# A feed-forward pass run over four chunks in two groups instead of over two chunks

## The chip, the cores and the metric

One Trainium2 chip, one core of it. The metric is device time in microseconds (us). The engines are TensorE (PE, matmuls; its weight loads are PEld), VectorE (DVE), ScalarE (ACT), GpSimd (POOL) and SyncE (SP, which here issues all DMAs). All arithmetic of this pass is in 32-bit floats.

## The reference

128 images are cut into 196 patches each, embedded to 256 features, and a class token is put in front: 197 tokens of 256. Then one layer: h + attention(layernorm(h)), and h + ffn(layernorm(h)). The feed-forward part is not the usual one:

```
global_context = x.mean(axis=1, keepdims=True)
gf = _global_net(global_context, ...)            # 256 -> 128 -> 64 -> 1, gelu, gelu, sigmoid
out = x
for _ in range(NUM_CYCLES):                      # 3
    tf = _coupling_net(out, ...)                 # 256 -> 256 -> 128 -> 64 -> 1, gelu x3, sigmoid
    combined = 0.7 * gf + 0.3 * tf
    coupling = BASE_COUPLING + adaptive_range * (combined - 0.5) * 2.0
    out = out + coupling * _twist(out)           # signed swap of the two halves of the features
return out
```

## The kernel before

The kernel has two passes. The first (embedding, attention, residual) goes image by image and writes its result to a DRAM scratch; the change leaves its code alone. The second pass is the feed-forward part. It works on **chunks** of two images: 2 x 197 = 394 columns (N2), features on the 128 partitions in two halves f. 64 chunks are taken in 32 **pairs**; c is 0 or 1.

Each engine has its own in-order program, written out by hand; semaphores tie them together, and nothing is scheduled by a planner. A chunk goes through these steps:

- SP loads the chunk twice from the scratch: `hl` for the norm, `hk` for the residual (L381).
- DVE `stats2` (L907, L911), POOL `norm2` (L525, L527), DVE `apply2` (L920) make the layer norm `hn2`.
- PE `x_transpose` (L1278) and ACT `x_copy` (L539) put it as `X`, features on partitions.
- DVE `gsums` (L925), then the global net: PE L1287, L1291, L1292 with ACT L649, L652, L655, and DVE `alphas` (L930).
- Three cycles of: layer 1 (PE L1307, eight records of two passes each for four matmuls), gelu (ACT L663); layer 2 (L1316), gelu (L667); layer 3 (L1321, 128 to 64), gelu (L671); layer 4 (L1325, 64 to 1, the weight column repeated 128 times so that every partition gets the result), tanh (L675). Then DVE `update`: four `base` instructions (L942) that don't need the tanh, and u (L946), new first half (L952), u (L953), new second half (L956).
- PE `y_transpose` (L1338), DVE `finish` (L965) adds it to `hk`, SP stores it (L391).

Chunk 1 runs about half a cycle behind chunk 0: PE does layers 3 and 4 of chunk 1 between layers 1 and 2 of chunk 0. Each chunk owns four of the eight PSUM banks. The order on each engine is that of its `pass2`, called for each pair.

## Time and profile before

| | us |
|---|---|
| median of 3 runs | 4073.27 |
| lowest, highest | 4049.71, 4074.95 |
| the profiled execution | 4066.9 |
| its span, first to last instruction | 4065.1 |
| PE busy | 3857.1 (95%) |
| DVE busy | 3042.6 (75%) |
| ACT busy | 2481.0 (61%) |
| POOL busy | 1818.8 (45%) |

The first pass ends near 2612 us. The rest is the second pass: a start of some 24 us in which the first two chunks are loaded and normed, and 32 pairs. Busy times of engines overlap and don't add up; which engine others wait for shows in the waits and in the timeline.

### The profile page before, as it was taken

What the parts mean: (1) busy time and instruction counts of PE and PEld (TensorE: products, weight loads), DVE (VectorE), ACT (ScalarE), POOL (GpSimd) and SP (SyncE); (2) the same over time, 40 slices, a digit from 0 to 9 for tenths busy, and PEclk for the clock granted to TensorE, in tenths of its full rate; (3) what the DMA queues carried; (4) which work ended last, traced back from release to release, by engine and by line L of the source; (5) the groups of instructions that cost most, each with busy time, mean ns of one, the idle gap of its engine ahead of it and who ended that gap; (6) DMA issues with size and microseconds to landing.
All of it is one profiled execution on the core that took longest, in us unless ns stands there. A gap on an engine that the chain in (4) does not pass through costs nothing.

```text
span 4065.1 us, 84521 instructions
## 1 busy us (share of the span) xinstructions
PE 3857.1 (95%) x29966; PEld 2761.4 (68%) x29966; DVE 3042.6 (75%) x7327; ACT 2481.0 (61%) x5890; POOL 1818.8 (45%) x2960
## 2 busy tenths in 40 slices
PE   6999999999999999999999999699999999999998
PEld 5888888888888888888888887444444444444444
DVE  6777777777777777777777777477777767777776
ACT  4777777777777777777777777444444444444443
POOL 3666666666666666666666666300000000000000
PEclk9999999999999999999999999799999999999999
DMA  3444444444444444444444444311112112111211
GB/s 106 127 127 127 122 122 123 126 127 124 125 128 128 123 122 122 124 128 126 126 128 126 122 123 105 83 48 57 48 60 59 50 52 60 56 48 60 60 49 40
DMA packets 199842, 398.21 MB, mean 98 GB/s; under 512 B 28032, under 2 KB 133760, under 8 KB 199424
## 3 DMA queue, kind: packets, MB, share of 16 engines
q1 hardware_dynamic: 199424, 392.81, 36.0%
q8 instruction: 242, 3.96, 0.4%
q14 instruction: 176, 1.44, 0.1%
HBM read 131.80 MB, written 53.26 MB: 46 GB/s over the span
## 4 chain that ended last, share of the span: by engine, by line
PE 81%; DVE 7%; issue 3%; ACT 3%; POOL 3%; DMA 2%; SPq 0%; DVEq 0%; POOLq 0%; ACTq 0%
PE ps L1307 13%; PE ps L1027 13%; PE ps L1316 7%; PE ps L1114 7%; PE ps L1062 6%; PE ps L1075 5%; PE ps L1325 4%; PE ps L1141 4%; PE ps L1321 3%; PE ps L1122 3%; PE ps L1099 3%; DVE mx L855 3%; PE ps L1148 3%; DVE mx L851 2%; PE ps L1143 2%
## 5 line engine op out<-in xcount | busy, mean ns | idle before, releaser
L1027 PE MATMUL ps<-xb,w_tok 128*128 128x196 f32 x3072 | 694.8, 350 | 0.8 <-DVE h L767 0.5
L851 DVE TENSOR_REDUCE mx<-ps 128x4 f32<-128x512 f32 x512 | 352.6, 689 | 362.6 <-PE ps L1143 362.6
L525 POOL TENSOR_SCALAR ve<-mv 128x4 f32<-128x4 f32 x64 | 14.9, 233 | 1286.8 <-DVE mv L911 1286.8
L1307 PE MATMUL ps<-X,cn_w 128*128 128x394 f32 x1536 | 552.6, 502 | 0.0
L855 DVE TENSOR_REDUCE mx<-ps 69x2 f32<-69x396 f32 x1024 | 528.8, 556 | 0.0
L545 ACT ACTIVATE p<-ps 128x394 f32<-128x394 f32 x1024 | 454.9, 499 | 78.1 <-PE ps L1075 68.6
L1027 PEld LDWEIGHTS ps<-xb,w_tok 128*128 128x128 f32 x3072 | 487.0, 190 | 1.2 <-DVE h L767 0.8
L663 ACT ACTIVATE a<-ps,cn_b 128x394 f32<-128x394 f32 x384 | 226.6, 590 | 368.4 <-PE ps L1307 354.8
L496 POOL TENSOR_TENSOR h<-h,att 128x256 f32<-128x256 f32 (+1 forms) x256 | 188.2, 755 | 533.3 <-DVE att L844 533.3
L1307 PEld LDWEIGHTS ps<-X,cn_w 128*128 128x128 f32 x1536 | 280.3, 191 | 176.3 <-issue 3.0
L1148 PE MATMUL ps<-kZ,qT 128*69 128x396 f32 x1024 | 398.4, 455 | 0.1
L1075 PE MATMUL ps<-qZ,kT 128*128 128x396 f32 (+1 forms) x2048 | 379.2, 318 | 12.9 <-DMA qZ<-mx_scratch 10.1
L457 POOL TENSOR_SCALAR_AFFINE_SELECT p<-p 128x512 f32<-128x512 f32 x512 | 372.1, 727 | 7.8 <-ACT p L545 7.8
L563 ACT ACTIVATE sq<-ps 128x256 f32<-128x256 f32 (+1 forms) x512 | 196.1, 383 | 280.9 <-PE ps L1062 280.8
L471 POOL TENSOR_TENSOR qkv<-qkv,wk_row 128x256 f32<-128x256 f32 (+1 forms) x256 | 229.3, 896 | 255.2 <-DVE qkv L819 255.2
L1075 PEld LDWEIGHTS ps<-qZ,kT 128*128 128x128 f32 (+1 forms) x2048 | 307.7, 167 | 39.6 <-issue 16.9
L1316 PE MATMUL ps<-a,cn_w 128*128 128x394 f32 x768 | 304.3, 518 | 10.4 <-DVE hk L965 6.3
L539 ACT ACTIVATE qkv<-ps 128x512 f32<-128x512 f32 (+1 forms) x512 | 306.3, 598 | 0.0
L539 ACT ACTIVATE qT<-ps 128x396 fp32r<-128x396 f32 x512 | 228.1, 499 | 118.2 <-PE ps L1114 118.1
L946 DVE SCALAR_TENSOR_TENSOR u<-X,c_tf,th 128x394 f32<-128x394 f32 x192 | 119.8, 624 | 224.9 <-ACT th L675 224.9
L1062 PE MATMUL ps<-w_qkv,hnT 64*128 64x256 f32 (+1 forms) x2048 | 284.0, 396 | 0.5 <-ACT hnT L539 0.5
L1099 PE MATMUL ps<-p,qkv 128*17 128x197 f32 x4096 | 254.1, 334 | 24.3 <-POOL p L461 18.9
(140 smaller groups left out, 8784.9 us busy)
## 6 DMA issues: line engine op xcount, KB each, us to landing
kZ<-kT SPq DMA_DIRECT2D x512, 198.0 KB, 3.6
qZ<-qT SPq DMA_DIRECT2D x256, 396.0 KB, 5.0
xb<-in_x SPq DMA_DIRECT2D x128, 588.0 KB, 6.5
h_scratch<-h SPq DMA_DIRECT2D x128, 128.0 KB
hl<-h_scratch SPq DMA_DIRECT2D x64, 256.0 KB
hk<-h_scratch SPq DMA_DIRECT2D x64, 256.0 KB
out<-hk SPq DMA_DIRECT2D x64, 256.0 KB
h_scratch<-h SPq DMA_DIRECT2D x128, 69.0 KB
```

The lines of the kernel that those rows point to most:

```text
L457: g.affine_select(out=v, in_=v, compare_op=ALU.is_ge, fill=0.0, base=0, pattern=[[0, HG], [1, P]], channel_multiplier=-1).then_inc(m_done, 1)
L539: return s.activation(o, i_, ACT.Copy)
L545: s.activation(p0[:, i, 2 * jj:2 * jj + 2, :], ps[:, (b0, b1)[jj], 0:2 * TE].rearrange("p (a b) -> p a b", b=TE)[:, :, 0:T], ACT.Exp).then ...
L851: v.tensor_reduce(mx[:, 0, 4 * i:4 * i + 4], ps[:, b0, :].rearrange("p (a b) -> p a b", b=P), AX.X, ALU.max, negate=True).then_inc(s_max, 1)
L855: v.tensor_reduce(mx[:T1, 1, 4 * i + 2 * jj:4 * i + 2 * jj + 2], ps[:T1, b, 0:2 * TE].rearrange("p (a b) -> p a b", b=TE), AX.X, ALU.max, ...
L1027: mm = t_.matmul(ps[:, W[ft], 0:NP], w_tok[:, k, ft * P:ft * P + P], xb[:, par, k, :], start=k == 0, stop=k == KT - 1)
L1062: mm = t_.matmul(bank[:, f], hnT[rows, f, t * P:t * P + M], w_qkv[rows, :, 4 * g:4 * g + 4, :].rearrange("p s h d -> p s (h d)"), start=Tr ...
L1075: mm = t_.matmul(ps[:M, b, x_ * 2 * N:x_ * 2 * N + 2 * N].rearrange("p (a b) -> p a b", b=N), kT[:, par, j, keys], qZ[:, :, j, queries], s ...
L1099: t_.matmul(ps[SLOT * i:SLOT * i + HD + 1, W[jj], j2 * T:j2 * T + T], qkv[:, r, 0, V, 4 * j + i, :], p0[:, j, i, :], start=True, stop=Fals ...
L1148: t_.matmul(bank, qT[:, j, P:T], kZ[:, :, j, :], start=True, stop=False)
L1307: mm = t_.matmul(ps[:, 4 * c + mt, 0:N2], cn_w1[:, f, mt * P:mt * P + P], X[:, c, state(cyc), f, :], start=f == 0, stop=f == FT - 1)
L1316: mm = t_.matmul(ps[:, 4 * c + 2, 0:N2], cn_w2[:, f, :], a1[:, c, f, :], start=f == 0, stop=f == 1)
```

## The change

The second pass takes 16 **quads** of four chunks (c is 0 to 3). Chunks 0 and 1 are group 0, chunks 2 and 3 group 1, and the groups run half a cycle apart. Each engine's program is a loop over `phases()`: in the phase of group G in cycle cyc, the other group O is in the second half of its own cycle ocyc (of quad oi).

- A chunk owns two banks (2c, 2c + 1); layer 2, layers 3 and 4 and the output transposes reuse those of layer 1.
- Layer 3 of a group's two chunks goes to array columns 0 to 63 and 64 to 127 (`tile_position`), into one bank; one gelu of 128 partitions makes `a3` of both. Layer 4 takes them as rows 0 to 63 and 64 to 127, with `cn_w4r` on both halves, into two banks.
- Layer 1 is issued in its two halves, layer 3 and layer 4 of the other group between them.
- The global net runs once for the four images of a group.
- DVE's `update` is split: `bases` of both chunks come first, then the next quad's norm work, then the rest of the update.
- SP loads all four `hl` before the four `hk` at the start, and within a quad both groups' `hl` ahead of the stores; the two stores of a group come ahead of its `hk` loads.
- Two small weight loads more at the kernel's start. `sq` and `qkv` move to the part of SBUF that the second pass reuses.

Of the diff, in the order helper, SP, ACT, DVE, PE:

```diff
+        def phases():
+            for i in range(QUADS):
+                for cyc in range(CYCLES):
+                    for G in range(2):
+                        oi, ocyc = (i, cyc) if G else (i, cyc - 1) if cyc else (i - 1, CYCLES - 1)
+                        yield i, cyc, G, oi, ocyc
...
+            def store_and_next_hk(i, G):
+                for c in (2 * G, 2 * G + 1):
                     store_out(i, c)
-                    sp.wait_ge(out_stored[c], i * 32 + 32)
-                    load2(hk, i + 1, c, hk_loaded)
+                if i + 1 < QUADS:
+                    for c in (2 * G, 2 * G + 1):
+                        sp.wait_ge(out_stored[c], i * 32 + 32)
+                        load2(hk, i + 1, c, hk_loaded)
+
+            for G in range(2):
+                next_hl(1, G)
+            for i in range(QUADS):
+                if i + 2 < QUADS:
+                    for G in range(2):
+                        next_hl(i + 2, G)
+                for G in range(2):
+                    store_and_next_hk(i, G)
...
+            def gelu3(i, cyc, G):
+                act.wait_ge(l3_done[G], i * CYCLES + cyc + 1)
+                s.activation(a3[:, G, :], ps[:, 4 * G + 1, 0:N2], ACT.Gelu, bias=cn_b3[:, 0:1]).then_inc(a3_ready[G], 1)
...
+            for i, cyc, G, oi, ocyc in phases():
+                O = 1 - G
+                fresh = ocyc == CYCLES - 1 and oi + 1 < QUADS
+                if oi >= 0:
+                    gelu3(oi, ocyc, O)
+                    if fresh:
+                        gnet(oi + 1, O, 1)
+                gelu1(i, cyc, 2 * G)
+                if oi >= 0:
+                    for c in (2 * O, 2 * O + 1):
+                        tanh(oi, ocyc, c)
+                    if fresh:
+                        gnet(oi + 1, O, 2)
+                gelu1(i, cyc, 2 * G + 1)
+                if oi >= 0 and ocyc == 1 and oi + 1 < QUADS:
+                    for c in (2 * O, 2 * O + 1):
+                        x_copy(oi + 1, c)
+                gelu2(i, cyc, 2 * G)
+                if cyc == CYCLES - 1 and i + 1 < QUADS:
+                    gnet(i + 1, G, 0)
+                gelu2(i, cyc, 2 * G + 1)
...
+            for i, cyc, G, oi, ocyc in phases():
+                O = 1 - G
+                pair = (2 * O, 2 * O + 1)
+                if oi >= 0:
+                    for c in pair:
+                        bases(oi, ocyc, c)
+                if i + 1 < QUADS:
+                    if cyc == 0:
+                        for c in (2 * G, 2 * G + 1):
+                            stats2(i + 1, c)
+                    elif cyc == 1:
...
+                                apply2(i + 1, c, False)
+                    elif cyc == 2:
+                        for c in (2 * G, 2 * G + 1):
+                            gsums(i + 1, c)
+                if oi >= 0:
+                    for c in pair:
+                        update(oi, ocyc, c)
+                    if ocyc == CYCLES - 1:
+                        if oi + 1 < QUADS:
+                            alphas(oi + 1, O)
+                        for c in pair:
+                            finish(oi, c)
...
+            def layer3(i, cyc, G):
+                for e in range(2):
+                    pe.wait_ge(a2_ready[2 * G + e], i * CYCLES + cyc + 1)
+                for e in range(2):
+                    mm = t_.matmul(ps[e * F3:e * F3 + F3, 4 * G + 1, 0:N2], cn_w3[:], a2[:, 2 * G + e, :],
+                                   start=True, stop=True, tile_position=(0, e * F3))
+                mm.then_inc(l3_done[G], 1)
+
+            def layer4(i, cyc, G):
+                pe.wait_ge(a3_ready[G], i * CYCLES + cyc + 1)
+                for e in range(2):
+                    rows = slice(e * F3, e * F3 + F3)
+                    t_.matmul(ps[:, 4 * G + 3 * e, 0:N2], cn_w4r[rows, :], a3[rows, G, :], start=True, stop=True)\
+                      .then_inc(l4_done[G], 1)
...
+            for i, cyc, G, oi, ocyc in phases():
+                layer1(i, cyc, 2 * G, 0)
...
+                    layer3(oi, ocyc, O)
...
+                layer1(i, cyc, 2 * G, 1)
+                if there_:
+                    layer4(oi, ocyc, O)
+                layer1(i, cyc, 2 * G + 1, 0)
...
+                layer1(i, cyc, 2 * G + 1, 1)
+                if there_ and ocyc == 1 and oi + 1 < QUADS:
+                    for c in (2 * O, 2 * O + 1):
+                        pe.wait_ge(th_ready[c], oi * CYCLES + ocyc + 1)
+                        x_transpose(oi + 1, c)
...
+                    y_transpose(oi, 2 * O)
+                layer2(i, cyc, 2 * G)
+                if there_ and ocyc == CYCLES - 1:
+                    y_transpose(oi, 2 * O + 1)
...
+                layer2(i, cyc, 2 * G + 1)
```

**The order on PE, layers 3 and 4.** PE before, in a plain cycle; the names are weights and inputs, so `a<-` stands for the activations, and `layer_ready` counts the gelus of a chunk:

```order
L1307 MATMUL ps<-X,cn_w 128x394 [waits x0_new_c0]
L1307 MATMUL ps<-X,cn_w 128x394
L1307 MATMUL ps<-X,cn_w 128x394 [waits x1_new_c0]
L1307 MATMUL ps<-X,cn_w 128x394
L1321 MATMUL ps<-a,cn_w 64x394 [waits g_ready_c1,layer_ready_c1]
L1316 MATMUL ps<-a,cn_w 128x394 [waits layer_ready_c0] x2
L1325 MATMUL ps<-a,cn_w4r 128x394 [waits layer_ready_c1]
L1321 MATMUL ps<-a,cn_w 64x394 [waits g_ready_c0,layer_ready_c0]
L1325 MATMUL ps<-a,cn_w4r 128x394 [waits layer_ready_c0]
```

PE after, one phase (group 0's layer 1, group 1's layers 3 and 4; `a3_ready` is the third gelu of a group):

```order
L1326 MATMUL ps<-X,cn_w 128x394 [waits x_ready_c0,x0_new_c0]
L1326 MATMUL ps<-X,cn_w 128x394
L1342 MATMUL ps<-a,cn_w 64x394 [waits a2_ready_c3,a2_ready_c2]
L1342 MATMUL ps<-a,cn_w 64x394
L1326 MATMUL ps<-X,cn_w 128x394 [waits x1_new_c0]
L1326 MATMUL ps<-X,cn_w 128x394
L1350 MATMUL ps<-a,cn_w4r 128x394 [waits a3_ready_g1]
L1350 MATMUL ps<-a,cn_w4r 128x394
L1326 MATMUL ps<-X,cn_w 128x394 [waits x_ready_c1,x0_new_c1]
L1326 MATMUL ps<-X,cn_w 128x394
L1326 MATMUL ps<-X,cn_w 128x394 [waits x1_new_c1]
L1326 MATMUL ps<-X,cn_w 128x394
```

Before, layer 4 of chunk 0 (the last row) stands right behind layer 3 of the same chunk; now a half of layer 1 stands between a group's layer 3 and its layer 4, and each is a pair of matmuls on half the array.

**The order on PE, output transposes.** PE before, where the last pair's second chunk is put out:

```order
L1321 MATMUL ps<-a,cn_w 64x394 [waits g_ready_c1,layer_ready_c1]
L1316 MATMUL ps<-a,cn_w 128x394 [waits layer_ready_c0,y_ready_c0]
L1316 MATMUL ps<-a,cn_w 128x394 [waits layer_ready_c0]
L1325 MATMUL ps<-a,cn_w4r 128x394 [waits layer_ready_c1]
L1321 MATMUL ps<-a,cn_w 64x394 [waits g_ready_c0,layer_ready_c0]
L1325 MATMUL ps<-a,cn_w4r 128x394 [waits layer_ready_c0]
L1338 MATMUL ps<-ident,X 128x128 [waits g_ready_c1,x1_new_c1,x0_new_c1]
L1338 MATMUL ps<-ident,X 128x128 x3
L1338 MATMUL ps<-ident,X 69x128 x4
L1307 MATMUL ps<-X,cn_w 128x394 [waits x_ready_c1]
```

PE after, the end of the phase in which group 1 of the last quad is put out (L1361 the output transposes, L1335 layer 2):

```order
L1326 MATMUL ps<-X,cn_w 128x394 x2
L1361 MATMUL ps<-ident,X 128x128 [waits x1_new_c2,x0_new_c2,g_ready_g1]
L1361 MATMUL ps<-ident,X 128x128 x3
L1361 MATMUL ps<-ident,X 69x128 x4
L1335 MATMUL ps<-a,cn_w 128x394 [waits a1_ready_c0] x2
L1361 MATMUL ps<-ident,X 128x128 [waits x1_new_c3,x0_new_c3]
L1361 MATMUL ps<-ident,X 128x128 x3
L1361 MATMUL ps<-ident,X 69x128 x4
L1335 MATMUL ps<-a,cn_w 128x394 [waits a1_ready_c1] x2
```

Each chunk's output transposes wait for its new state as before; they now stand ahead of a layer 2 of the other group, and layer 1 waits for the bank's last reader, where layer 2 did.

**The order on DVE.** DVE before, in the second cycle (L942 base, L946 to L956 the rest of an update, L925 sums for the global net):

```order
L942 SCALAR_TENSOR_TENSOR base<-X,alpha 128x197 [waits alpha_ready_c0]
L942 SCALAR_TENSOR_TENSOR base<-X,alpha 128x197 x3
L946 SCALAR_TENSOR_TENSOR u<-X,c_tf,th 128x394 [waits layer_ready_c0]
L952 TENSOR_TENSOR X<-base,u 128x394 [waits u0_ready_c0,base_ready_c0]
L953 SCALAR_TENSOR_TENSOR u<-X,c_tf,th 128x394
L956 SCALAR_TENSOR_TENSOR X<-base,u 128x394 [waits u1_ready_c0]
L925 TENSOR_REDUCE gsum<-X 128x4 [waits x_ready_c0]
L942 SCALAR_TENSOR_TENSOR base<-X,alpha 128x197 [waits alpha_ready_c1]
L942 SCALAR_TENSOR_TENSOR base<-X,alpha 128x197 x3
L946 SCALAR_TENSOR_TENSOR u<-X,c_tf,th 128x394 [waits layer_ready_c1]
L952 TENSOR_TENSOR X<-base,u 128x394 [waits u0_ready_c1,base_ready_c1]
```

DVE after, the phase of group 0's second cycle (L952 base, L926 the next quad's norm, L962 on the rest of the updates):

```order
L952 SCALAR_TENSOR_TENSOR base<-X,alpha 128x197 [waits x_ready_c2,alpha_ready_g1]
L952 SCALAR_TENSOR_TENSOR base<-X,alpha 128x197 x3
L952 SCALAR_TENSOR_TENSOR base<-X,alpha 128x197 [waits x_ready_c3,alpha_ready_g1]
L952 SCALAR_TENSOR_TENSOR base<-X,alpha 128x197 x3
L926 TENSOR_SCALAR hn<-hl,mv,rstd 128x256 [waits x_transposed_c0,rstd2_g0]
L926 TENSOR_SCALAR hn<-hl,mv,rstd 128x256
L926 TENSOR_SCALAR hn<-hl,mv,rstd 69x256 x2
L926 TENSOR_SCALAR hn<-hl,mv,rstd 128x256 [waits x_transposed_c1,rstd2_g0]
L926 TENSOR_SCALAR hn<-hl,mv,rstd 128x256
L926 TENSOR_SCALAR hn<-hl,mv,rstd 69x256 x2
L962 SCALAR_TENSOR_TENSOR u<-X,c_tf,th 128x394 [waits th_ready_c2]
L968 TENSOR_TENSOR X<-base,u 128x394 [waits u0_ready_g1,base_ready_g1,y_transposed_c2]
```

The bases of both chunks now come ahead of the norm work, and both chunks' updates behind it; only the updates wait for the tanh.

## Rows read from the trace of the kernel before

**Rows 1.** Windows: length, busy PE PEld DVE ACT POOL (count), clock, DMA share, GB/s.
```profile
2680.00:4050.00 1370.00, 1272.04 (x4427) 643.32 (x4426) 991.01 (x2451) 620.64 (x1230) 76.06 (x120) 1.00 0.18 54
...
4058.00:4062.00 4.00, 1.94 (x8) 1.58 (x8) 1.37 (x3) 0.00 (x0) 0.00 (x0) 0.50 0.21 68
```

**Rows 2.** Timeline of PE: start us, length us, instruction, count.
```profile
2690.08 2.81 PE L1307 MATMUL ps<-X,cn_w 128*128 128x394 f32 x8
```

**Rows 3.** Waits, 3000 to 3500 us: us in total, times, longest.
```profile
DVE u L946 <- ACT th L675: 72.6, 23, 4.8
...
PE ps L1325 <- ACT a L671: 22.3, 33, 0.7
```

**Rows 4.** Timeline of PE, about one pair.
```profile
3207.28 0.50 PE L1287 MATMUL ps<-gsum,gc_w 128*128 128x2 f32 x4
3207.64 1.57 PE L1316 MATMUL ps<-a,cn_w 128*128 128x394 f32 x4
3209.14 0.38 PE L1292 MATMUL ps<-ga,gc_w3r 64*128 64x2 f32 x2
...
3209.66 2.92 PE L1307 MATMUL ps<-X,cn_w 128*128 128x394 f32 x8
...
3220.57 1.06 PE L1338 MATMUL ps<-ident,X 128*128 128x128 f32 x8 [0.80 <-issue]
3221.47 2.81 PE L1307 MATMUL ps<-X,cn_w 128*128 128x394 f32 x8
...
3225.80 2.81 PE L1307 MATMUL ps<-X,cn_w 128*128 128x394 f32 x8
3228.54 0.88 PE L1321 MATMUL ps<-a,cn_w 128*64 128x394 f32 x2
3229.35 1.59 PE L1316 MATMUL ps<-a,cn_w 128*128 128x394 f32 x4
3230.87 0.93 PE L1325 MATMUL ps<-a,cn_w4r 64*128 64x394 f32 x2
3231.73 0.88 PE L1321 MATMUL ps<-a,cn_w 128*64 128x394 f32 x2
```

**Rows 5.** Timeline of PE, tiled groups in the first pass.
```profile
1514.90 0.53 PE L1099 MATMUL ps<-p,qkv 128*17 128x197 f32 x8
1515.24 0.31 PE L1103 MATMUL ps<-p,qkv 69*17 69x69 f32 x8
...
1518.95 1.14 PE L1062 MATMUL ps<-w_qkv,hnT 64*128 64x256 f32 x8
1520.01 0.50 PE L1141 MATMUL ps<-kZ,qT 128*128 128x256 f32 x2
```

**Rows 6.** Timeline, DVE's rows at the same pair.
```profile
3221.31 1.28 DVE L965 TENSOR_TENSOR hk<-hk,ps 128x512 f32<-128x512 f32 x2 [0.64 <-PE ps L1338]
...
3222.51 1.42 DVE L942 SCALAR_TENSOR_TENSOR base<-X,alpha 128x197 f32<-128x197 f32 x4
...
3223.85 0.62 DVE L946 SCALAR_TENSOR_TENSOR u<-X,c_tf,th 128x394 f32<-128x394 f32 x1
...
3226.23 1.39 DVE L907 BATCH_NORM_STATS2 st<-hl 128x6 f32<-128x256 f32 x4
...
3229.88 1.34 DVE L920 TENSOR_SCALAR hn<-hl,mv,rstd 128x256 f32<-128x256 f32 x4
```

**Rows 7.** Timeline, start and end of the second pass.
```profile
2614.52 0.78 SPq L381 DMA_DIRECT2D hl<-h_scratch  x2
...
2625.65 1.40 DVE L907 BATCH_NORM_STATS2 st<-hl 128x6 f32<-128x256 f32 x4 [3.85 <-DMA hl<-h_scratch]
...
2636.67 3.72 PE L1307 MATMUL ps<-X,cn_w 128*128 128x394 f32 x6
...
4051.42 1.06 PE L1338 MATMUL ps<-ident,X 128*128 128x128 f32 x8
...
4058.15 1.94 PE L1338 MATMUL ps<-ident,X 128*128 128x128 f32 x8 [3.25 <-DVE X L956]
```

More of the change, by code:

```diff
@@ L708, in _ @@
+            for c in range(4):
                 x_copy(0, c)
             for l in range(3):
-                for c in range(2):
-                    gnet(0, c, l)
-            pairs(act, pass2)
-            layer(PAIRS - 1, 1, CYCLES - 1, 2)
-            layer(PAIRS - 1, 1, CYCLES - 1, 3)
+                for G in range(2):
+                    gnet(0, G, l)
+            for i, cyc, G, oi, ocyc in phases():
[19 more added lines that the diff above has]
+                gelu2(i, cyc, 2 * G + 1)
@@ L717, in _ @@
+            gelu3(QUADS - 1, CYCLES - 1, 1)
+            for c in (2, 3):
+                tanh(QUADS - 1, CYCLES - 1, c)
         @block.vector
@@ L992, in _ @@
-            for c in range(2):
+            for c in range(4):
                 stats2(0, c)
-            for c in range(2):
+            for c in range(4):
                 apply2(0, c, True)
-            for c in range(2):
+            for c in range(4):
                 gsums(0, c)
-            for c in range(2):
-                alphas(0, c)
-            pairs(dve, pass2)
-            finish(PAIRS - 1, 0)
-            update(PAIRS - 1, 1, CYCLES - 1, False)
-            finish(PAIRS - 1, 1)
+            for G in range(2):
+                alphas(0, G)
@@ L1006, in _ @@
+            for c in (2, 3):
+                bases(QUADS - 1, CYCLES - 1, c)
+                update(QUADS - 1, CYCLES - 1, c)
+            for c in (2, 3):
+                finish(QUADS - 1, c)
         @block.tensor
@@ new lines, in layer2 @@
+            def layer2(i, cyc, c):
+                n = i * CYCLES + cyc
+                for f in range(2):
+                    pe.wait_ge(a1_ready[c], n * 2 + f + 1)
+                    mm = t_.matmul(ps[:, 2 * c, 0:N2], cn_w2[:, f, :], a1[:, c, f, :], start=f == 0, stop=f == 1)
+                mm.then_inc(l2_done[c // 2], 1)
+            def layer3(i, cyc, G):
[5 more added lines that the diff above has]
+                mm.then_inc(l3_done[G], 1)
@@ L1374, in _ @@
[L1374 removed]
+            for c in range(4):
                 x_transpose(0, c)
+            for c in range(4):
+                pe.wait_ge(x_ready[c], 2)
             for l in range(3):
[L1377 to L1383 removed]
+                for G in range(2):
+                    gnet(0, G, l)
```

415 lines of the change are left out of this document (164 added, 251 removed).

## The prediction

> **What bounds the kernel now.** I read the windows view first, since the change touches only the feed-forward pass (the second pass). Between 2680 and 4050 us TensorE (PE) is busy 1272 of 1370 us at granted clock 1.00, VectorE (DVE) 991, ScalarE (ACT) 621 [rows 1]. PE is the bound. The period comes from the timeline: the layer-1 group that follows the second chunk's output transposes starts at 2690.08 [rows 2] and, 12 pairs later, at 3221.47 [rows 4], so a pair of chunks costs 44.28 us, and two pairs, which is what one pass of the new loop (a quad) covers, 88.56.
>
> PE's timeline over one pair [rows 4] shows the price of each group, read from start to next start: layer 1 of a chunk 25.80 to 28.54 = 2.74; layer 2 29.35 to 30.87 = 1.52; layer 3 28.54 to 29.35 = 0.81; layer 4 30.87 to 31.73 = 0.86; output transposes of a chunk 20.57 to 21.47 = 0.90; the global net of a chunk 0.36 + 0.52 = 0.88 (3207.28 to 3207.64, then two small groups from 3209.14 to 3209.66). It also shows where PE stands idle: the first chunk's layer 4 comes right behind its own layer 3 and waits 0.68 for the third gelu, once a cycle (the waits view: 22.3 us in 33 times [rows 3]), and 0.80 stand before the second output transposes. That is 3 x 0.68 + 0.80 = 2.8 us of a pair.
>
> **Layers 3 and 4 of two chunks side by side.** A full-array matmul record of 394 columns takes 2.74/8 = 0.34. Layer 3 now uses 64 array columns for each of two chunks, layer 4 64 array rows. The first pass already does both kinds. Column tiles: eight records of 197 columns on four tiles take 1514.90 to 1515.24 = 0.34, where one after the other they would take 8 x 0.17 = 1.37, so four do run abreast. Row tiles: eight of 256 columns on two tiles take 1518.95 to 1520.01 = 1.06 against 8 x 0.22 = 1.77, so abreast with some start cost [rows 5]. I take the new pair of layer 3 at one old one, 0.81, and of layer 4 at 0.86: the saving is 0.81 + 0.86 = 1.67 for each cycle of two chunks, 6 cycles a quad: **-10.0 us a quad**. Bounds: by the row tiles' ratio (0.6 of serial) layer 4's pair costs 1.03, +0.17, or +1.0 a quad; if neither overlaps, the saving is 0.
>
> A rule speaks against it. The Trainium skill, TensorEngine Tiling (Array Packing), Key Properties, says that a change of tiling mode drains TensorE. Layer 3 and layer 4 stand alone between full-array groups, so this is four changes a phase. By that rule, with 0.15 a change, a quad would pay 24 x 0.15 = 3.6. The trace bounds it from the side: 128*64 and 64*128 groups before exceed 2 x 0.34 by 0.13 and 0.18, which their price already holds [rows 4].
>
> **The stagger.** What was a chunk half a cycle behind another is now a group of two behind a group of two. In one phase PE issues: layer 1 of G's first chunk, half; layer 3 of the other group O; layer 1, other half; layer 4 of O; layer 1 of the second chunk; layer 2 twice. Walk it from its start: layer 3 ends at 1.4 + 0.8 = 2.2, the third gelu with its handoff, 0.68 by the idle it caused before, is done by 2.9 while layer 1 runs to 3.6, so layer 4 waits for nothing. The six waits of 0.68 in two pairs go, and the 0.80 before the second transposes with them: **-5.6**. Next late is the following: layer 4 ends at 4.5, the two tanh, at some 0.6 to 0.68 each behind two gelus on ACT, at 5.3 and 5.9, and DVE's update can start at 5.4.
>
> DVE's load does not fall: 991/1370 x 88.56 = 64.1 us a quad busy, some 66 with its short gaps. A phase of DVE is two bases (1.34 each, 3222.51 to 3223.85), two updates (2.38 each, 3223.85 to 3226.23) = 7.4, and norm or output work: the statistics of two chunks 3.65 (3226.23 to 3229.88), the finish of a chunk 1.20 (3221.31 to 3222.51) [rows 6], the rest of the 66 shared over the third to sixth phase. That order, bases and norm work ahead of the updates, fills the time until the tanh. Phase by phase (PE / DVE): first, with the old group's output, 12.8 / 13.8; second 10.3 / 11.1; third 10.3 / 10.0; fourth, with transposes, 11.7 / 10.0; fifth 12.0 / 9.3; sixth, with output, 13.1 / 12.0. DVE is behind PE by at most a microsecond or so, and PE needs the second chunk's new state only some 5 us into the next phase, so plain phases cover that. Not covered are the two phases with output: there PE reaches the output transposes at 7.8 and the first chunk's update ends at about 8.2, and DVE's finish in turn waits for the second transposes. I take 0.9 for both: **+0.9**. Layer 1 is now cut in two by layer 3 and 4, 12 more starts of groups; a start costs 0.1 to 0.18 by the excess above: **+1.5** (range 0 to 3.6).
>
> **The global net** runs once for four images, not once for two: 2 x 0.88 less on PE, **-1.8** (DVE loses two alphas, off the path). Input and output transposes, layer 1 and layer 2 keep their number. Period: 88.56 - 10.0 - 5.6 + 0.9 + 1.5 - 1.8 = 73.6. The phase walk alone sums to 71 before the extra starts, 72.5 with them. I take **73.0**, times 16 quads = 1168 against 1417.
>
> **Edges.** Before, the first layer 1 starts at 2636.67, 11.0 after the second chunk's norm data land at 2625.65, the third of four loads (0.4 MB each) since 2614.5 [rows 7], so roughly 100 to 125 GB/s. Four chunks of hl come first now; the fourth lands near 2630, +4.5. The next quad's hl queues behind four hk loads, and the first phase's DVE work asks for it; with 3.2 MB ahead of it I allow +4 (range 0 to 8). Two more small weight loads at the start, +0.9. The first quad has no older group and the last no successor: -9 over both. The tail: before, from the end of the last layer 2, where the transposes start at 4051.42 [rows 7], to the end at 4065.1 = 13.7; now DVE updates two chunks there, one base, one update and one finish more (4.9): 18.6. So 2636.7 + 4.5 + 4 + 0.9 + 1168 - 9 + 18.6 = 3823.7, and 1.8 outside the span as before (4066.9 against 4065.1): 3825. The profiled run lies 6 under the median of the three, so I say **3830** us, 6.0% less. Loads ahead of stores on SP I cost at nothing: no wait of DVE for hl or hk stands in the steady rows, and each load has over 20 us before it is read; without that cover a quad's first norm would stand some 5 us, 80 in all. The first pass keeps its order on every engine; moved tiles cost nothing.
>
> **Rivals.** *Not side by side.* The two halves of a 32-bit matmul go to the same tile and could hold the next tile back. Then 10.0 a quad are not saved: +160, 3990; half of it 3910. The first pass's times [rows 5] speak against, though with smaller tiles. *DVE's handoff decides.* DVE waits for the tanh each phase and its norm work comes late in others; if its 66 us plus a wait of 2 in each phase add up in a row, a quad takes 78: +80, 3910. For it: DVE waited for tanh 72.6 us of 500 before [rows 3]. Against: it now has work to do ahead of the wait. *No stalls at all:* 70.5 a quad, 3790. *The clock, slower than before:* in the phases with output PE waits for DVE. At the end of the kernel, after PE had idled 3.25 us, the granted clock is 0.50 and eight transpose records keep PE busy 1.94 instead of 1.06 [rows 1, 4, 7]. If the waits in those two phases were long enough for the clock to stay at 1.2 GHz through them (25 us of PE work a quad), a quad gains 25 us, +400: 4230. It is slower than now by 1% from 18 us of such work a quad. Against: idles of 0.68 and 0.80 left the clock at 1.00 for 1370 us.
>
> **How the numbers follow.** Forecast 3800 to 3870: 66%. Half or no overlap, 3880 to 3990: 12%. DVE's handoff, 3870 to 3930: 13%. Under 3800: 6%. Clock, over 4110: 3%. The range 3785 to 3930 leaves out about 2 in 10. Within 1% is what a measurement of this kernel cannot tell from no change (the three runs lie 0.6% apart); nearly no case ends there. Faster 0.95, same 0.02, slower 0.03.
>
> **What would show it.** In the profile after: the start-to-start time from layer 3 to the other half of layer 1 about 0.8 (1.5 if not side by side), the same for layer 4; no wait of layer 4 for the third gelu; period of a quad 73; waits of PE for DVE only at the output transposes, under 1 us each; DVE busy 88 to 91% of the steady stretch, PE 95% or more; clock 1.00. It is wrong if tiles of 64 columns do not overlap, or if DVE's updates reach PE late in plain phases.

## The result and the profile after

| | before | after |
|---|---|---|
| median, us | 4069.32 (4 runs) | 3770.72 (4 runs) |
| lowest, highest | 4049.71, 4074.95 | 3767.47, 3772.90 |
| profiled execution, its span | 4066.9, 4065.1 | 3769.01, 3767.3 |
| PE busy | 3857.1 (95%) | 3644.8 (97%) |
| DVE busy | 3042.6 (75%) | 3028.1 (80%) |
| ACT busy | 2481.0 (61%) | 2402.5 (64%) |

The ratio is 0.927 (95% interval 0.924 to 0.931): 7.3% less, where 6.0% was forecast. The first pass is unchanged: its last store is issued at 2612.17 before and at 2612.20 after. So everything happened in the 1452.9 us between that store and the end of the span, which are now 1155.1.

The windows view of the changed kernel, 1000 us of the steady part. Columns: window, its length, busy us of PE, PEld, DVE, ACT and POOL, the granted clock, the DMA engines' mean share, GB/s.

```profile
2700.00:3700.00 1000.00, 993.03 (x3919) 531.26 (x3916) 906.81 (x2254) 508.26 (x976) 86.37 (x112) 1.00 0.23 69
```

Beside [rows 1]: PE goes from 93% to 99% of the stretch, DVE from 72% to 91%, ACT stays at half. PE is still the bound, with DVE not far behind. The clock is 1.00 on the mean, as before. Before, that mean hides two short falls, at 3308.7 and at 4018.7, of about 3.4 us each. Of the first, from the trace of before, a window and PE's row:

```profile
3308.00:3313.00 5.00, 4.20 (x15) 3.01 (x14) 3.77 (x9) 0.59 (x1) 0.00 (x0) 0.66 0.44 134
3309.14 1.94 PE L1338 MATMUL ps<-ident,X 128*128 128x128 f32 x8 [0.80 <-issue]
```

PE had idled no longer there than in every other pair (0.20, 0.68 and 0.80), and eight transpose records take 1.94 instead of 1.06. The pair lasts 45.73 instead of 44.28. The changed kernel has no such fall between 2647 and 3752.

The period, from PE's timeline of the changed kernel (start, duration, engine and line, operation, out<-in, array shape, data in, count; a wait stands in brackets at the end). The two rows are the first layer of group 0's global net, once a quad, 13 quads apart:

```profile
2693.87 0.50 PE L1308 MATMUL ps<-gsum,gc_w 128*128 128x4 f32 x4
...
3598.36 0.50 PE L1308 MATMUL ps<-gsum,gc_w 128*128 128x4 f32 x4
```

904.49 / 13 = 69.58 us for a quad, where two pairs took 88.56 [rows 2, 4].

PE's timeline, one plain phase (3010.38 to 3020.39) and parts of the two phases with output (from 3043.74 and from 3056.75, to 3069.92):

```profile
3010.38 1.49 PE L1326 MATMUL ps<-X,cn_w 128*128 128x394 f32 x4
3011.80 0.88 PE L1342 MATMUL ps<-a,cn_w 128*64 128x394 f32 x4
3012.61 1.59 PE L1326 MATMUL ps<-X,cn_w 128*128 128x394 f32 x4
3014.13 0.93 PE L1350 MATMUL ps<-a,cn_w4r 64*128 64x394 f32 x4
3014.99 2.92 PE L1326 MATMUL ps<-X,cn_w 128*128 128x394 f32 x8
3017.74 2.81 PE L1335 MATMUL ps<-a,cn_w 128*128 128x394 f32 x8
3020.39 1.49 PE L1326 MATMUL ps<-X,cn_w 128*128 128x394 f32 x4
...
3043.74 1.49 PE L1326 MATMUL ps<-X,cn_w 128*128 128x394 f32 x4
...
3056.75 1.49 PE L1326 MATMUL ps<-X,cn_w 128*128 128x394 f32 x4
...
3065.32 1.06 PE L1361 MATMUL ps<-ident,X 128*128 128x128 f32 x8 [0.48 <-DVE X L972]
3066.22 1.49 PE L1335 MATMUL ps<-a,cn_w 128*128 128x394 f32 x4
...
3069.92 1.48 PE L1326 MATMUL ps<-X,cn_w 128*128 128x394 f32 x4
```

Layer 3 of two chunks costs 3011.80 to 3012.61 = 0.81, exactly what that of one chunk cost in [rows 4]. Layer 4 of two chunks costs 3014.13 to 3014.99 = 0.86, again the old price of one. So the two array halves work side by side without any loss. Layer 1 in halves costs 1.42 + 1.52, where it costs 2.75 in one piece (3014.99 to 3017.74). Two layers 2 back to back take 2.65 (3017.74 to 3020.39), which is eight records of 0.331 with nothing between. PE waits once in a quad, 0.48 before the first output transposes of the second such phase (3065.32).

The waits view of the changed kernel, 3000 to 3500 (total us, number of waits, longest):

```profile
DVE u L962 <- ACT th L688: 25.4, 14, 2.7
...
PE ps L1361 <- DVE X L972: 3.3, 7, 0.5
```

The wait of layer 4 for the third gelu, 22.3 us in 33 times before [rows 3], is no longer in the list. DVE's wait for the tanh fell from 72.6 us to 25.4.

Summed over a quad from start to start, group by group:

| us for a quad (before: two pairs) | before | after |
|---|---|---|
| layer 1 | 33.7 | 34.8 |
| layer 2 | 17.8 | 16.4 |
| layers 3 and 4 | 20.6 | 9.8 |
| input and output transposes | 6.7 | 6.4 |
| global net | 3.7 | 1.7 |
| PE's waits | 6.1 | 0.5 |
| sum | 88.6 | 69.6 |

The ends, from the timeline of the changed kernel: the first hl load, DVE's statistics of the fourth chunk, the first two phases' starts, and the tail.

```profile
2614.55 5.84 SPq L390 DMA_DIRECT2D hl<-h_scratch  x8
...
2628.63 1.40 DVE L913 BATCH_NORM_STATS2 st<-hl 128x6 f32<-128x256 f32 x4 [1.04 <-DMA hl<-h_scratch]
...
2642.05 7.74 PE L1326 MATMUL ps<-X,cn_w 128*128 128x394 f32 x16 [0.40 <-issue]
...
2652.27 1.49 PE L1326 MATMUL ps<-X,cn_w 128*128 128x394 f32 x4
...
3746.53 1.49 PE L1335 MATMUL ps<-a,cn_w 128*128 128x394 f32 x4
3748.79 0.88 PE L1342 MATMUL ps<-a,cn_w 128*64 128x394 f32 x4 [0.77 <-ACT a L680]
...
3754.54 1.94 PE L1361 MATMUL ps<-ident,X 128*128 128x128 f32 x8 [3.25 <-DVE X L972]
```

The fourth chunk's statistics start at 2628.63 and the first layer 1 at 2642.05, 5.4 later than before [rows 7]. In the tail PE waits 0.77 and 3.25, and behind the 3.25 the eight transpose records take 1.94 instead of 1.06. Two more waits in the tail are not shown: 0.68 before layer 4 and 1.75 before the last transposes. The granted clock is 0.50 (1.2 GHz) from 3754 to 3760, just as before [rows 1, 7].

### The profile page after: what moved, and what is told of

The parts are those of the page before. It is cut to its first block, busy times and chain, and to the rows that moved or that the text cites. A ratio compares the mean times of both kernels' runs of the same rounds, so it can differ in the third digit from the quotient of the medians.

```text
span 3767.3 us, 83941 instructions
## 1 busy us (share of the span) xinstructions
PE 3644.8 (97%) x29710; PEld 2685.5 (71%) x29710; DVE 3028.1 (80%) x7295; ACT 2402.5 (64%) x5698; POOL 1830.5 (49%) x2960
## 3 DMA queue, kind: packets, MB, share of 16 engines
q1 hardware_dynamic: 199584, 392.81, 38.4%
## 4 chain that ended last, share of the span: by engine, by line
PE 81%; DVE 9%; issue 3%; POOL 3%; ACT 2%; DMA 2%; SPq 0%; DVEq 0%; POOLq 0%; ACTq 0%
PE ps L1048 14%; PE ps L1326 11%; PE ps L1135 8%; PE ps L1083 7%; PE ps L1335 6%; PE ps L1096 6%; PE ps L1162 4%; PE ps L1120 4%; PE ps L1169 4%; PE ps L1143 3%; PE ps L1164 3%; PE ps L1350 2%; PE ps L1342 2%; POOL p L473 2%; PE ps L1058 1%
## 5 line engine op out<-in xcount | busy, mean ns | idle before, releaser
L1326 PE MATMUL ps<-X,cn_w 128*128 128x394 f32 x1536 | 584.9, 510 | 0.4 <-issue 0.4
L1335 PE MATMUL ps<-a,cn_w 128*128 128x394 f32 x768 | 281.8, 499 | 0.0
L1120 PE MATMUL ps<-p,qkv 128*17 128x197 f32 x4096 | 253.9, 334 | 23.3 <-POOL p L473 18.6
L952 DVE SCALAR_TENSOR_TENSOR base<-X,alpha 128x197 f32<-128x197 f32 x768 | 264.7, 417 | 0.0
```

Source lines behind the costliest of these rows:

```text
L1120: t_.matmul(ps[SLOT * i:SLOT * i + HD + 1, W[jj], j2 * T:j2 * T + T], qkv[:, r, 0, V, 4 * j + i, :], p0[:, j, i, :], start=True, stop=Fals ...
L1326: mm = t_.matmul(ps[:, 2 * c + mt, 0:N2], cn_w1[:, f, mt * P:mt * P + P], X[:, c, state(cyc), f, :], start=f == 0, stop=f == FT - 1)
L1335: mm = t_.matmul(ps[:, 2 * c, 0:N2], cn_w2[:, f, :], a1[:, c, f, :], start=f == 0, stop=f == 1)
```

## The experiments

Twelve runs follow: ten new kernels, the changed kernel again (9) and kernel 10 again (12). The first pass, which none of them changes, issues its last store between 2604.6 and 2617.2 us depending on the execution, so whole times of different executions compare to some ten us only. The ratios are to the kernel before, run beside each experiment; its median there lies between 4049.6 and 4071.1, and one and the same kernel has the ratio 0.925 in 10 and 0.929 in 12, so ratios of different experiments don't compare to better than half a per cent. Periods of a quad (start to start over 10 to 13 quads) and the **second pass's length** (from the last store of the first pass to the end of the span) compare far better (the changed kernel has 1155.1 and, in experiment 9, 1155.5), and I use those, each from one profiled execution. Theory A in the expectations is the one held when they were written; in experiment 2 the prediction's account is rival B. Experiments 4 to 7 are one execution each.

**1. Without side by side.** Layers 3 and 4 of a group's two chunks run one after the other at the array's usual position, with a gelu each; the stagger stays.

```diff
-                    mm = t_.matmul(ps[e * F3:e * F3 + F3, 4 * G + 1, 0:N2], cn_w3[:], a2[:, 2 * G + e, :],
-                                   start=True, stop=True, tile_position=(0, e * F3))
-                mm.then_inc(l3_done[G], 1)
+                    t_.matmul(ps[:F3, 4 * G + 1 + 2 * e, 0:N2], cn_w3[:], a2[:, 2 * G + e, :],
+                              start=True, stop=True).then_inc(l3_done[G], 1)
...
```

> The stagger without the side by side: layer 3 and layer 4 of the two chunks one after the other at the full array's position, with two gelus of 64 partitions between. In the changed kernel a quad takes 69.55 us, layer 3 of two chunks 0.81, layer 4 0.86. Theory A (TensorE alone sets the period): each phase gains 1.67, a quad 10.0, so 79.6 a quad and 3770 + 160 = 3930 us. Rival B (VectorE, busy 91% of the steady stretch, sets part of the period): the serial matmuls fill TensorE's own waits first, so clearly less, +7 a quad or 3885. Rival C (the stagger was worth nothing by itself): back to the 88.56 of before, over 4050.

Measured: 3876.49 us (3871.26 to 3877.19), ratio 0.957 (0.9555 to 0.9583). The period is 76.37, +6.8. PE's timeline of this kernel, a plain phase:

```profile
3044.13 1.49 PE L1328 MATMUL ps<-X,cn_w 128*128 128x394 f32 x4
3045.54 1.54 PE L1344 MATMUL ps<-a,cn_w 128*64 128x394 f32 x4
3047.01 1.59 PE L1328 MATMUL ps<-X,cn_w 128*128 128x394 f32 x4
3048.53 1.59 PE L1350 MATMUL ps<-a,cn_w4r 64*128 64x394 f32 x4
3050.05 2.92 PE L1328 MATMUL ps<-X,cn_w 128*128 128x394 f32 x8
...
3055.46 1.49 PE L1328 MATMUL ps<-X,cn_w 128*128 128x394 f32 x4
```

Layer 3 of two chunks takes 1.47 (3045.54 to 3047.01) and layer 4 1.52 (3048.53 to 3050.05). The second matmul adds only 0.66 to a first one of 0.81 or 0.86, which is two records at 0.33. So side by side saves 0.66 twice, 1.3 a phase and not 1.67. Over six phases that is 7.9 a quad. The changed kernel's wait of 0.48, gone here, takes part of it back, and another 0.6 comes back at the output transposes: layer 2 between the two of a phase takes 1.45 to 1.47 in the changed kernel and 1.32 here, the piece of layer 1 ahead of them 1.48 or (without the wait) 1.59 and 1.43 here, the transposes 0.90 and 0.87. These look like idles for DVE too short for the list, which no run shows directly. So theory B's mechanism, serial matmuls that fill TensorE's own waits, is worth 1.1 of the 3.2 by which 10.0 was too much. The other 2.1 are the price: theory A compared with two groups that stand apart. Where the old kernel ran layer 3 of a chunk alone between full-array groups, the price was not the matmul's alone. Of the 19.0 us a quad, 12.2 come from what is left here: the order, the stagger and the global net run once for four images.

**2. Layer 1 whole.** Layer 3 goes behind the whole layer 1 of the first chunk, layer 4 behind that of the second.

```diff
                 layer1(i, cyc, 2 * G, 0)
+                layer1(i, cyc, 2 * G, 1)
                 if there_:
...
                     layer3(oi, ocyc, O)
...
-                layer1(i, cyc, 2 * G, 1)
+                layer1(i, cyc, 2 * G + 1, 0)
+                layer1(i, cyc, 2 * G + 1, 1)
                 if there_:
                     layer4(oi, ocyc, O)
```

> Layer 1 of each chunk whole again: layer 3 of the other group behind the first chunk's layer 1, layer 4 behind the second's. Theory A (what a group costs over its floor comes with a change of array shape, not with the number of groups; room between VectorE and TensorE matters): plain phases stay within 0.1 of 10.0 us, tanh and updates come 2.9 us later, and TensorE waits some 2.5 us more for VectorE in each of the two phases with output: +5 a quad, 3850 us. Rival B (each group start costs 0.1 to 0.18, as the prediction had it): 6 to 12 fewer starts, -1 to -1.8 a quad, 3745 to 3755.

Measured: 3926.21 us (3921.97 to 3926.69), ratio 0.969 (0.9675 to 0.9708); period 79.8, +10.2. PE's timeline of this kernel around the output transposes, and the windows view beside it:

```profile
3021.84 0.28 PE L1313 MATMUL ps<-ga,gc_w3r 64*128 64x4 f32 x2
3025.25 1.94 PE L1361 MATMUL ps<-ident,X 128*128 128x128 f32 x8 [3.14 <-DVE X L972]
3026.99 2.83 PE L1335 MATMUL ps<-a,cn_w 128*128 128x394 f32 x4
3029.61 1.73 PE L1361 MATMUL ps<-ident,X 128*128 128x128 f32 x8
```

```profile
3024.00:3029.00 5.00, 3.75 (x12) 2.82 (x13) 4.67 (x9) 0.21 (x1) 0.00 (x0) 0.52 0.00 0
```

The tanh comes late, DVE updates late, and PE waits 3.14 us for the updated X (3025.25). The mean granted clock from 3024 to 3029 is 0.52, so 1.2 GHz for nearly all of it: eight transpose records take 1.94 instead of 1.06, the next layer 2 takes 2.83 where the one in the changed kernel takes 1.49. Theory A had the sign and half of the size. Summed over a quad, PE's waits grow from 0.5 to 7.6 (two of 3.14 before the output transposes, two of 0.68 for the tanh before the input transposes), which is more than A's 5. The slower clock takes some 3.4 more, in the output transposes and the layers 2 between them. This is the prediction's clock rival at work, in a kernel whose waits are 3 us and not 0.5. On B this run does not decide: layer 1 does cost 1.2 less a quad (33.5 against 34.8), but layer 2 behind layer 4 costs more, and the global net's last layer now stands beside layer 4 and pays no round trip of its own; experiments 5 to 7 decide. The order with layer 1 in two pieces is what keeps the waits away.

**3. Bases with each update**, behind the norm work as before, not ahead of it.

```diff
-                if oi >= 0:
-                    for c in pair:
-                        bases(oi, ocyc, c)
...
                     for c in pair:
+                        bases(oi, ocyc, c)
                         update(oi, ocyc, c)
```

> VectorE's split undone: each chunk's four base instructions stand again directly ahead of its own update, behind the norm work. Theory A (the bases ahead of the tanh are what keeps the updates early): phases with little norm work see the second chunk's update 1.3 us later; plain phases absorb that, the output phases show it as a wait of TensorE: +1.3 to 1.8 a quad, 3790 to 3800 us. Rival B (TensorE sets the period whatever VectorE's order): 3770, period 69.5.

Measured: 3798.37 us (3796.39 to 3801.36), ratio 0.938 (0.9365 to 0.9393); period 71.65, +2.1. PE's timeline of this kernel, the end of a phase with output:

```profile
3001.89 1.49 PE L1333 MATMUL ps<-a,cn_w 128*128 128x394 f32 x4
3004.69 1.06 PE L1359 MATMUL ps<-ident,X 128*128 128x128 f32 x8 [1.30 <-DVE X L972]
```

Theory A holds, with a little more than its 1.3 to 1.8. PE now waits 1.30 before the second transposes, in both phases with output, and the 0.48 before the first ones is gone. Plain phases hide the 2.7 us of late bases, these two don't, as the prediction said of DVE. The clock stays at full speed behind a wait of 1.30.

**4. Loads at the start as before**, hl and hk in turn for each chunk.

```diff
             for c in range(4):
                 load2(hl, 0, c, hl_loaded)
-            for c in range(4):
                 load2(hk, 0, c, hk_loaded)
```

> At the start of the second pass the loads for the norm and for the residual alternate chunk by chunk, as before the change. In the changed kernel the four norm loads land 2.9 us apart, the last at 2628.6. Theory A (the fourth norm load gates the start): it lands as the seventh of eight, near 2637, the first layer 1 starts 9 us later, 3779 us. Rival B (the start is gated by norm, transposes and the global net): no difference. The period of a quad stays 69.55 in both.

Measured: 3777.2 us in one run, period unchanged at 69.58. The timeline of this kernel (the first load's issue, the first layer 1):

```profile
2613.38 0.78 SPq L390 DMA_DIRECT2D hl<-h_scratch  x2
...
2649.45 6.12 PE L1325 MATMUL ps<-X,cn_w 128*128 128x394 f32 x9 [0.40 <-issue]
```

The last store of the first pass is issued at 2611.03 here, so the first layer 1 starts 38.4 behind it, against 29.85 in the changed kernel: +8.6, and the second pass is 1164.5 against 1155.1. As theory A had it, loading all four hl first is worth 9 us, once. The other half of the SP edit, hl ahead of the stores within a quad, was not run. By the programs' order, with the stores first SP waits for a finish that stands on DVE behind the norm of the data that SP has yet to load, and the kernel would never end.

**5 to 7. What does a group's start cost?** The prediction charged 0.1 to 0.18 for each group that starts. Three kernels issue one group more in each phase without output (4 a quad), its result unused: 5, layer 3's pair again right behind itself; 6, the same pair between the two halves of the second chunk's layer 1; 7, a full-array layer 2 in that same place. The output is not changed by it, the work is. The two functions, `twice3` of 5 and 6 and `twice2` of 7:

```diff
+            def twice3(G):
+                for e in range(2):
+                    t_.matmul(ps[e * F3:e * F3 + F3, 4 * G + 2, 0:N2], cn_w3[:], a2[:, 2 * G + e, :],
+                              start=True, stop=True, tile_position=(0, e * F3))
...
+            def twice2(G):
+                for f in range(2):
+                    t_.matmul(ps[:, 4 * G + 2, 0:N2], cn_w2[:, f, :], a1[:, 2 * G, f, :], start=f == 0, stop=f == 1)
```

> The changed kernel with layer 3's pair of matmuls issued twice, the second time right beside the first, into a free bank that nobody reads; in the four phases of a quad without output. Measures what a pair on half arrays costs without a start of its own. Theory A (the excess over 2 x 0.33 comes once per run of equal groups, at its ends): the double takes 0.66 more in each of those phases, period +2.6, 72.2. Rival B (the excess belongs to each pair of tiles, not to the change of shape): +0.81 a phase, +3.2 a quad.

Measured: 3817.02 us in one run, period 72.19, +2.6. PE's timeline of this kernel:

```profile
3031.21 0.88 PE L1342 MATMUL ps<-a,cn_w 128*64 128x394 f32 x4
3031.92 0.83 PE L1348 MATMUL ps<-a,cn_w 128*64 128x394 f32 x4
3032.68 1.59 PE L1326 MATMUL ps<-X,cn_w 128*128 128x394 f32 x4
```

The two pairs take 1.47 (3031.21 to 3032.68) where one took 0.81: the second costs 0.66, so two records at 0.33, with no start. That is theory A's number.

> The same second pair of layer 3, in the same four phases, but set apart between the two halves of the second chunk's layer 1. Theory A: it pays its two changes, 0.81 for itself and some 0.1 for layer 1's extra end: +0.90 a phase, +3.6 a quad, 1.0 a quad more than beside. Rival B: the same as beside it, within 0.2 a quad.

Measured: 3837.28 us in one run, period 73.58, +4.0. The same of this kernel:

```profile
3028.83 1.59 PE L1326 MATMUL ps<-X,cn_w 128*128 128x394 f32 x4
3030.35 0.88 PE L1348 MATMUL ps<-a,cn_w 128*64 128x394 f32 x4
3031.16 1.59 PE L1326 MATMUL ps<-X,cn_w 128*128 128x394 f32 x4
3032.59 2.81 PE L1335 MATMUL ps<-a,cn_w 128*128 128x394 f32 x8
```

The halves and the pair between them take 3.76 (3028.83 to 3032.59) against 2.75 for layer 1 in one piece. By the period it is +1.00 a phase, 0.34 more than the same work beside its like, as theory A had it.

> At the same place a full-array group instead: the first chunk's layer 2 of the other group once more (four records, 1.33 by the floor of 0.331 a record), into the free bank. It tells a change of array shape from any change of group. Theory M (only a change of array shape costs, by the rule of the drain): +1.33 to 1.40 a phase, +5.3 to 5.6 a quad, and layer 1's halves take 1.33 to 1.40 each. Rival N (any group of other operands costs at its start): 1.33 + 0.2, +6.1 or more a quad.

Measured: 3852.89 us in one run, period 74.84, +5.3. The same of this kernel:

```profile
3030.60 1.59 PE L1326 MATMUL ps<-X,cn_w 128*128 128x394 f32 x4
3032.03 1.49 PE L1348 MATMUL ps<-a,cn_w 128*128 128x394 f32 x4
3033.35 1.49 PE L1326 MATMUL ps<-X,cn_w 128*128 128x394 f32 x4
3034.67 2.81 PE L1335 MATMUL ps<-a,cn_w 128*128 128x394 f32 x8
```

4.07 (3030.60 to 3034.67) against 2.75: +1.32, which is four records at 0.331 and nothing else, though the group has other weights, other data, another bank and a neighbour on each side that it cuts in two. So a start costs nothing, and of the theories here the one that only changes of array shape cost is left. What costs is the round trip from the full array to half-array shapes and back: 0.34 in experiment 6, and (10.01 - 28 x 0.331) / 2 = 0.37 for each of the two in a plain phase of the changed kernel. The Trainium skill, TensorEngine Tiling (Array Packing), Key Properties, says that a change of tiling mode drains TensorE. These three runs agree as far as the time goes, 0.34 for the round trip and nothing for a change of weights or of bank; that it is a drain, no run shows.

**8 and 9. The ends.** Kernel 8 starts group 0 as soon as its two chunks are normed, with group 1's transposes and global net inside the first phase, and in the tail makes both bases ahead of the last two updates. Kernel 9 is the changed kernel again, on the same chip.

```diff
-            for c in range(4):
+            for c in (0, 1):
                 x_transpose(0, c)
...
+            for f in range(FT):
+                layer1(0, 0, 0, f)
+            for c in (2, 3):
+                x_transpose(0, c)
...
             for c in (2, 3):
                 bases(QUADS - 1, CYCLES - 1, c)
+            for c in (2, 3):
                 update(QUADS - 1, CYCLES - 1, c)
```

> The changed kernel with its two ends tightened: group 0 starts as soon as its own two chunks are normed and its global net is done, group 1's transposes and global net lie inside the first phase; at the end both chunks' bases come ahead of the two last updates. Theory (both ends are chains of waits, and the steady part is untouched): the first layer 1 starts near 2636 instead of 2642, the second phase near 2647 instead of 2652.3, the tail is 1.3 shorter: 6 us less than the changed kernel on the same chip, period 69.55. Rival (TensorE at the lower clock at the start gives part of it back, group 1's norm comes late): 1 to 3 us.

> The changed kernel itself on the chip of the run before, for a comparison of the two: period 69.55, 6 us above the version with tightened ends by the theory, and the ratio to the kernel before near 0.927 again.

Measured: 3767.97 us (3766.62 to 3774.22) and 3771.82 (3769.80 to 3776.28), ratios 0.926 (0.9247 to 0.9272) and 0.927 (0.9256 to 0.9282). By whole times no difference can be claimed. By the second pass's length it is 1151.3 against 1155.5: 4.2 less where 6 was expected, 3.0 at the start, where PE now waits 1.17 for DVE once, and 1.3 in the tail. That lies between the theory and its rival (1 to 3).

**10. One round trip fewer.** Kernel 8 with the last small layer of the global net, also a half-array shape, right behind layer 4 instead of in a place of its own.

```diff
                     layer4(oi, ocyc, O)
+                    if fresh:
+                        gnet(oi + 1, O, 2)
                 layer1(i, cyc, 2 * G + 1, 0)
-                if there_ and fresh:
-                    gnet(oi + 1, O, 2)
                 layer1(i, cyc, 2 * G + 1, 1)
```

> The version with tightened ends, and the global net's last matmul (64 rows by 128 columns, as layer 4) directly behind layer 4 instead of between the halves of layer 1. Theory M (each excursion out of the full array costs some 0.34 over its floor, as the second pair of layer 3 set apart showed against the one beside): one excursion less in each of the two phases with output, less the waits for VectorE that this uncovers there; period 69.55 - 0.3 to 0.6, 5 to 10 us in all, 3758 to 3763 where the tightened ends gave 3768. Rival (TensorE waits for VectorE in those phases anyway): period within 0.1 of 69.55.

Measured: 3765.03 us (3763.18 to 3767.88), ratio 0.925 (0.924 to 0.9266), but the period is 69.58 and the second pass 1151.1 against kernel 8's 1151.3: nothing gained. Of the 3.4 us between the two profiled executions, 3.2 are the first pass. PE's timeline of this kernel, the two phases with output:

```profile
3043.98 2.92 PE L1343 MATMUL ps<-X,cn_w 128*128 128x394 f32 x8
3047.19 1.06 PE L1378 MATMUL ps<-ident,X 128*128 128x128 f32 x8 [0.29 <-DVE X L982]
...
3057.01 2.92 PE L1343 MATMUL ps<-X,cn_w 128*128 128x394 f32 x8
3060.79 1.06 PE L1378 MATMUL ps<-ident,X 128*128 128x128 f32 x8 [0.87 <-DVE X L982]
```

The round trip is saved, and PE waits for DVE instead: 0.29 and 0.87 before the first transposes of each phase, where the changed kernel has one wait of 0.48. So in these two phases DVE sets the time, which experiment 11 tries. The rival was right.

**11 and 12. DVE's work moved out of the way.** Kernel 10 with the statistics of the next quad's chunk 1 taken out of the first phase, which has the old group's output, and put into the second. Kernel 12 is kernel 10 again, on the same chip.

```diff
                     if cyc == 0:
-                        for c in (2 * G, 2 * G + 1):
+                        for c in ((1, 2, 3) if G else (0,)):
                             stats2(i + 1, c)
```

> The version with the global net's matmul moved, and VectorE's norm statistics of the second chunk taken out of the first phase, where TensorE waits 0.87 for VectorE, into the second, which has no output. Theory (in the phases with output VectorE's chain of bases, statistics and updates sets the time): the first chunk's update starts at the tanh, 5.5 instead of 6.3 into the phase, the wait falls from 0.87 to 0.1 to 0.3, the second phase stays at 10.0 since TensorE reads the new state late; period 69.0, 9 us below the version without it. Rival (VectorE falls behind in the second phase and TensorE waits there): period 69.5 or more.

> The version before it again, on the same chip, for the comparison: period 69.55, TensorE's waits before output transposes 0.29 and 0.87.

Measured: 3757.37 us (3750.16 to 3762.88) and 3760.26 (3757.74 to 3764.67), ratios 0.927 (0.9259 to 0.9286) and 0.929 (0.9273 to 0.9299); periods 68.99 and 69.59, second pass 1143.1 and 1151.4. PE's timeline of kernel 11, the phase whose wait was 0.87:

```profile
3056.22 2.92 PE L1343 MATMUL ps<-X,cn_w 128*128 128x394 f32 x8
3059.43 1.06 PE L1378 MATMUL ps<-ident,X 128*128 128x128 f32 x8 [0.29 <-DVE X L982]
```

The wait is down to 0.29, and 0.6 a quad is saved. By whole times no difference can be claimed, since their ranges overlap. In the two profiled executions they are 3757.38 and 3757.74, but the first pass of kernel 11's ended 8 us later (2612.56 against 2604.60). By the second pass's length this is the best version: 8.3 less than kernel 12 (9 was expected) and 12.0 less than the changed kernel, 4.2 from the ends and the rest from the period.

## Why the prediction was right, and where it missed

The direction, the bound (PE, clock 1.00) and the two sources of the gain were right. The time, 3770.7, lies 14 us under the low end of the range. The span was forecast at 3823.7 and is 3767.3, 56.4 less: the period carries (73.0 - 69.58) x 16 = 54.7, the +4 for the queue fell away, first and last quad saved 1.6 less and the tail took 0.8 more.

- **Layer 1 cut in two: "12 more starts of groups", +1.5.** This is the step that failed. The excess of 0.13 and 0.18 over two records was read right in [rows 4], but put down to a start, of which the change has more. A cut by itself costs nothing (experiment 7). The excess is the price of a change of array shape (experiments 5 and 6), and those became fewer. Before, a cycle of a pair goes full, layer 3, full, layer 4, layer 3, layer 4, full: six changes, 36 in two pairs. Now a phase goes full, layer 3, full, layer 4, full: four, 24 a quad. At 0.17 to 0.19 a change (half of a round trip) the 12 fewer are 2.0 to 2.3. (The price of going straight from layer 4's shape to layer 3's was not measured by itself; in [rows 4] layer 4 costs 0.86 there too.) But these 2.1 were in the sum already: the -10.0 takes the six dropped pairs of groups away at their whole price, excess and all. The right term was 0 and not +1.5, which is 24 of the 54.7 us. Without it the forecast would have been 3806, inside the range and still too high.
- **What no term had.** The terms sum to 73.6 and the quad takes 69.6: of the 4.0 between, 1.5 are the starts and 0.9 the waits, and 1.6 remain (0.2 of them in the global net's own row). Two things in the traces are of that size; no experiment took them apart. One is the global net's half-array layers, which make 12 changes of shape of their own in two pairs before and 4 in a quad now, up to 1.4. The other is short idles. Before, the second chunk's layer 1 is followed directly by the layer 2 of the same chunk, which needs its gelus, and takes longer than ahead of another group:

```profile
3013.46 2.86 PE L1307 MATMUL ps<-X,cn_w 128*128 128x394 f32 x8
3016.35 1.59 PE L1316 MATMUL ps<-a,cn_w 128*128 128x394 f32 x4
```

That is 2.89, and 2.93 from 3044.34 to 3047.27, where the same layer ahead of another group takes 2.70 (3018.46 to 3021.16): 0.8 in two pairs. The new order has another group in between, but loses 0.6 at the output transposes (experiment 1).
- **Rounding, 71 to 72.5 to 73.0.** The terms summed to 73.6 and the walk without extra starts to 71; I took 73.0. The bare walk was off by 1.4 only.
- **Side by side, -10.0.** The layers' own time fell 10.8 (20.6 to 9.8), near the forecast, and the prices taken for the pairs, 0.81 and 0.86, were exact. As an account of the cause it is too much: side by side saves 24 records of 0.331, 7.9, and the other 2.1 are the changes of shape above. Undone alone, it gives back 6.8 (experiment 1).
- **The waits, -5.6 and +0.9.** Measured 6.1 to 0.5, -5.6 in all. I had left out the 0.20 of smaller waits a pair, and DVE's lateness in the phases with output is one wait of 0.48, not 0.9 (though part of the 0.6 above may be the same lateness). That it is DVE's order that keeps this small holds (experiment 3), and so does that layer 4 waits for nothing with a piece of layer 1 ahead of it. That the pieces must be halves for the tanh to come early shows in experiment 2.
- **Global net, -1.8:** measured 3.7 to 1.7.
- **DVE** is busy 90.7% of the steady stretch; 88 to 91 was forecast.
- **The ends.** The fourth chunk's data came at 2628.6 (forecast 2630), the first layer 1 at 2642.05 (forecast 2642.1). That it is so near is partly luck: 0.9 of the forecast was for the small weight loads, and the first pass ends at 2612.2 in both profiled executions. The +4 for the next quad's hl was not there: the second phase starts at 2652.27, 10.2 behind the first, as long as a plain one. First and last quad save 7.4 and not 9. The tail, from the last layer 2 to the end, is 19.4 against 18.6.
- **Loads ahead of stores cost nothing,** as forecast, as far as the trace goes: from 2700 to 3700 no wait for hl or hk stands in the waits view. The order at the start earns 9 us (experiment 4), which the prediction had only as a smaller loss.
- **The rivals.** "Not side by side" is excluded by the two prices. "DVE's handoff" is not what happened, but is the next limit: saving PE a round trip in a phase with output brings nothing until DVE's work moves (experiments 10 and 11). "No stalls at all", 3790 at 70.5 a quad, was nearest and still 19 too high. The clock rival did not happen at 0.48 of wait and did at 3.14 (experiment 2). What was said against it, that idles of 0.68 and 0.80 left the clock at 1.00 for 1370 us, was read off a mean: it fell twice in that stretch, for 3.4 us each, and the pair of the first lasted 1.45 longer.

## What to carry to other kernels

Where groups of matmuls of different array shapes alternate, count the changes of shape, not the groups: put all work of the small shape side by side and back to back, and cut large full-array groups where it helps, since a cut by itself costs nothing and only a change of shape does. Let the other stream's work, cut into pieces, stand between a short matmul and the next one that needs its activation, and on the engine that comes second (here DVE) put what doesn't need the late operand ahead of what does. Before pricing a new order by an excess seen in the old one, find out which transition pays it, count that transition in both, and see that no other term of the sum has taken it already.

## What the runs showed of the hardware that was not expected

- Two 32-bit matmuls with 64 array columns each, and two with 64 array rows each, take the time of one, to 0.01 us, although each is two records (0.81 and 0.86 a pair; 0.66 for one more pair beside).
- A full-array group with other weights, input and bank between two halves of another group costs its records at 0.331 us and nothing more (experiment 7); a round trip to half-array shapes costs 0.34 to 0.37 us.
- The granted clock stayed at 1.00 with waits of PE of 1.30 us twice a quad (experiment 3) and fell to 0.50 around each wait of 3.14 and 3.25 us (experiment 2 and the tail), where a layer 2 group then took 2.83 instead of 1.49. The length of a single wait does not decide alone: in the kernel before it also fell twice, at 3308.7 and 4018.7, with no wait over 0.80 near, and did not at the same waits of the other pairs.
- The first pass, the same code in all these kernels, issued its last store between 2604.6 and 2617.2 us from one execution and chip to the next: more than several of the edits here change.
